# A transformer block in fp32 on one core: the scores of the first key block on 64-row halves of TensorE, interleaved with those of the second

## The chip, the cores and the metric

The kernel runs on one core of a Trainium2 chip. A core has five engines that run side by side and wait for one another by semaphores: TensorE (PE in the profile; its weight loads are listed apart as PEld), VectorE (DVE), ScalarE (ACT), GpSimd (POOL) and SyncE (SP, which here issues the DMAs). The metric is the time of one execution on the device, in microseconds.

## The reference

Sixteen sequences of 256 tokens with 128 features go through a pre-norm block: causal attention with 16 heads (key width 8, value width 64) and then a mixture of 8 experts, in which each expert takes its 64 best tokens of a sequence. What the change touches is the attention:

```python
scores = jnp.einsum('bhqd,bhkd->bhqk', q, k) / scale
causal = jnp.triu(jnp.ones((T, T), dtype=bool), k=1)
scores = jnp.where(causal, jnp.asarray(-jnp.inf, scores.dtype), scores)
attn = jax.nn.softmax(scores, axis=-1)
ctx = jnp.einsum('bhqk,bhkd->bhqd', attn, v)
out = ctx.transpose(0, 2, 1, 3).reshape(B, T, HEADS * D_V)
return out @ Wo
```

## The kernel before, in words

The attention is cut into 64 units: unit `u = 4 b + j` is head group `j` (four heads) of sequence `b`. The work of a unit is spread over several steps of a software pipeline, and every engine has its own program, written out by hand: `batch(b, par)` loops over `j`, and in step `u` the engine works on units `u + 2` to `u - 3`. The order of instructions on an engine is the order in that function; there is no scheduler. Sequences 4 to 9 run in a loop on the device, the others are unrolled.

On TensorE, step `u` of the kernel before does in this order: the scores of the second query block (queries 128 to 255 against all 256 keys) of unit `u + 1`, the query and key products of sequence `b + 2` (only at `j == 3`), the first eight transposes of the probabilities of unit `u - 1` (`turn`), small products of the norms and the gate, the contexts of unit `u - 2`, the output projection of unit `u - 3`, the last four transposes (`turn_last`), the value product of unit `u + 2`, and the scores of the first query block (queries 0 to 127 against keys 0 to 127) of unit `u + 2`. So the first block's scores at the end of one step stand directly ahead of the second block's scores of the same unit at the start of the next.

The scores of four heads come out of one contraction over 128 rows: queries and keys are split into high and low parts, 32 rows a head, and the keys lie in a block diagonal, `k_diag`. The first block is one matmul over all 128 rows with 512 columns, into `s0_ps` (L1276). It adds to the causal mask that VectorE has written there (L892, semaphore `filled0`). The second block is two matmuls over 64 rows each with 512 columns, one on the lower and one on the upper half of the array, for two heads each, into `s1_ps` (L1189), and then four small bf16 matmuls that add the causal mask, also on halves (L1194).

Behind the scores stands this loop: `s0_done` releases VectorE's maximum (L939), this the exponentials of the first block on ScalarE (L529, `exp0`), behind which ScalarE copies transposed probabilities (L538). Those of the second block follow (`s1_done`, maximum L883, L529, `exp1`). TensorE may overwrite `s1_ps` for the next unit only after `exp1`, and `s0_ps` only when VectorE has filled it anew behind `exp0`. The value products, the query and key products and the small products of norms and gate share one tile, `misc_ps0`: each waits until the one before has been copied out (`v_ready`, `qk_lo_done`, `gate_ready`, `x2T_ready`).

Of the kernel before, what the change touches and what calls it, by code (L numbers as in the profile page):

```python
# [13 lines left out]
P = 128  # L14
B, T, D = 16, 256, 128
TB = T // P
H, DK, DV = 16, 8, 64
HG = 4
# [47 lines left out]
def block_kernel(nc, x, w_q, w_k, w_v, w_o, gate_w, w1, w2, out):  # L66
# [3 lines left out]
    with ExitStack() as ctx:  # L70
# [6 lines left out]
        def sem(name):  # L77
            return ctx.enter_context(nc.semaphore(name))
# [149 lines left out]
        v_done = sem("v_done")  # L228
        v_ready = sem("v_ready")
        s0_done = sem("s0_done")  # L230
        s1_done = sem("s1_done")
# [445 lines left out]
        def _(dve):  # L677
# [199 lines left out]
            def batch(b, par):  # L877
                for j in range(G):
# [12 lines left out]
                    if has(u + 2, UNITS) and has(u + 1, UNITS):  # L891
                        nc.vector.tensor_copy(s0_ps[:, :, :], bcast(causal[:, :], 1, HG)).then_inc(filled0, 1)  # L892
                    if j == 0 and has(b + 2, B):
# [12 lines left out]
                    if j == 3 and has(b - 1, B):  # L906
                        norm2_stats(b - 1)
                    if j == 0 and has(b - 2, B):
                        norm2(b - 2)
                    if j == 0 and has(b - 3, B):  # L910
                        if at(u, (44,)):
                            dve.wait_ge(probsT_done[0], 1)
                        copy_gate(b - 3, misc_ps[0])
                        if at(u, (44,)):
                            copy_probs(0, misc_ps[0][0:HALF, T:2 * T])
                    if j == 1 and has(b - 2, B):
# [12 lines left out]
                    if j == 2 and has(b - 2, B):  # L929
                        split_xg(b - 2)  # L930
                    if has(u - 2, UNITS):
                        copy_context(u - 2, r2)
# [97 lines left out]
        def _(pe):  # L1030
# [147 lines left out]
            def batch(b, par):  # L1178
                for j in range(G):
                    u = b * G + j  # L1180
                    r1, r2, rm = (j + 1) % RING, j % RING, (j + 1) % RING
                    if has(u + 1, UNITS):
                        q, kb = (j + 1) % G, par if j < 3 else 1 - par
                        if isinstance(u, int) and u == -1:
                            pe.wait_ge(halves, 10)
                        await_count(pe, exp1, u + 1)
                        tiles = ((slice(0, HALF), 0), (slice(HALF, P), 2))
                        for rows, i in tiles:
                            nc.tensor.matmul(s1_ps[:, i:i + 2, :], qT[kb][rows, q, P:T], k_diag[kb][rows, q, i:i + 2, :],  # L1189
                                             start=True, stop=False, skip_group_check=True)  # L1190
                        for half in range(2):
                            cols = slice(P + half * HALF, P + (half + 1) * HALF)
                            for rows, i in tiles:
                                last = nc.tensor.matmul(s1_ps[:, i:i + 2, cols], half_rows[rows, half, :],  # L1194
                                                        bcast(half_masks[rows, half, :], 1, 2),
                                                        start=False, stop=(half == 1), skip_group_check=True)
                        last.then_inc(s1_done, 1)
                    if j == 3 and has(b + 2, B):
# [8 lines left out]
                        last.then_inc(qk_done, 1)  # L1207
                    if has(u - 1, UNITS):
                        turn(u - 1, rm)
                    if j == 0 and has(b - 3, B):  # L1210
# [55 lines left out]
                    if has(u + 2, UNITS):  # L1266

                        q, kb = (j + 2) % G, par if j < 2 else 1 - par
                        if isinstance(u, int) and u == -2:
                            pe.wait_ge(first_loaded, QK_LOADS)  # L1270
                        elif j == 2 or (isinstance(u, int) and u == -1):
                            pe.wait_ge(qk_loaded, QK_LOADS * (b + 2))
                        await_count(pe, filled0, u + 2)
                        if isinstance(u, int) and u == -2:
                            nc.tensor.matmul(s0_ps[:, :, :], ident_bf[:, :], bcast(causal[:, :], 1, HG), start=True, stop=True)
                        nc.tensor.matmul(s0_ps[:, :, :], qT[kb][:, q, 0:P], k_diag[kb][:, q, :, 0:P], start=False, stop=True,  # L1276
                                         skip_group_check=True).then_inc(s0_done, 1)

# [95 lines left out]
```

## Time and profile before

| | |
|---|---|
| median of 3 runs | 560.72 us (559.99 to 560.88) |
| the profiled execution, its own time | 560.4 us |
| its span from first to last instruction | 558.7 us |
| busy share PE / PEld / DVE / ACT / POOL | 94% / 76% / 74% / 72% / 45% |
| granted clock of TensorE, mean of the span | 0.993 |

The span is the stretch in which the instructions lie; 1.7 us of the execution's own time lie around it. A busy share is a mean over the whole span; attention takes the larger part of it and the experts the rest, and the engines are not loaded alike in the two. Matmuls are pipelined: the start of one is often earlier than the end of the one ahead, so what a matmul costs TensorE is read from start to start, and its own duration tells when its result is there.

### The profile page before, as it was taken

The page shows a single profiled execution, that of the slowest core. Times are in us where ns is not written, and L with a number is a line of the kernel's source. Part 1 is how long each engine was busy: PE and PEld are TensorE (multiplying, and loading weights), DVE is VectorE, ACT ScalarE, POOL GpSimd, SP SyncE. Part 2 cuts the span into 40 slices and gives each one's busy share as a digit, 9 for nine tenths or more (in the row PEclk, how much of TensorE's full clock was granted, in tenths as well). Part 3 has the DMA queues.
Part 4 walks back from the last instruction along what each step waited for, and adds up shares of the span by engine and source line. Part 5 has one row for each costly group of instructions (what it writes and reads, how often), then busy time and mean ns, then how long its engine had stood idle before and what let it go on. Part 6 is the DMA issues. An engine that isn't in the chain of part 4 may idle for free.

```text
span 558.7 us, 13959 instructions
## 1 busy us (share of the span) xinstructions
PE 527.9 (94%) x4777; PEld 427.2 (76%) x4777; DVE 415.7 (74%) x1066; ACT 403.8 (72%) x1383; POOL 253.5 (45%) x249
## 2 busy tenths in 40 slices
PE   1389999999999999999999999999999999999996
PEld 1257777777777877877777777777789998999995
DVE  1477888888888888888898999899873776542354
ACT  4688888888888988989889888889745434334230
POOL 5165555555556556565565565556820101011011
PEclk9979999999999999999999999999999999999999
DMA  4585251732544225042250523410300011000011
GB/s 122 150 211 154 53 151 52 230 118 58 149 117 113 77 73 150 24 126 76 76 149 16 142 76 77 131 22 29 106 21 1 2 39 59 20 21 11 11 29 49
DMA packets 49783, 45.97 MB, mean 82 GB/s; under 512 B 4288, under 2 KB 46528, under 8 KB 49728
## 3 DMA queue, kind: packets, MB, share of 16 engines
q1 hardware_dynamic: 48864, 44.60, 29.2%
q8 instruction: 32, 0.52, 0.4%
q10 hardware_dynamic: 864, 0.66, 0.4%
q14 instruction: 23, 0.19, 0.1%
HBM read 26.35 MB, written 18.89 MB: 81 GB/s over the span
## 4 chain that ended last, share of the span: by engine, by line
PE 90%; ACT 4%; DVE 4%; issue 1%; DMA 1%; POOL 0%; ACTq 0%; DVEq 0%; POOLq 0%
PE ctx_ps L1075 16%; PE misc_ps L1084 12%; PE t_ps L1162 10%; PE t_ps L1048 6%; PE t_ps L1058 5%; PE t_ps L1049 5%; PE s_ps L1189 4%; PE misc_ps L1034 4%; PE s_ps L1146 4%; PE misc_ps L1036 3%; PE misc_ps L1035 3%; PE s_ps L1147 3%; PE s_ps L1148 3%; PE s_ps L1276 3%; PE ctx_ps L1172 2%; ACT prob L529 2%
## 5 line engine op out<-in xcount | busy, mean ns | idle before, releaser
L529 ACT ACTIVATE prob<-s_ps,neg_max 128x128 f32<-128x128 f32 (+1 forms) x512 | 209.9, 437 | 21.2 <-DVE neg_max L939 18.2
L489 POOL TENSOR_TENSOR probn<-prob,inv 128x1024 f32<-128x1024 f32 x64 | 121.2, 1893 | 56.3 <-DVE inv L960 56.3
L529 ACT ACTIVATION_READ_ACCUMULATOR prob<-s_ps,neg_max 128x1 f32 x512 | 114.5, 224 | 0.0
L482 POOL TENSOR_TENSOR probn<-prob,inv 128x512 f32<-128x512 f32 x64 | 66.5, 1040 | 77.7 <-PE t_ps L1058 69.6
L883 DVE TENSOR_REDUCE neg_max<-s_ps 128x4 f32<-128x1024 f32 x64 | 76.4, 1193 | 0.8 <-PE s_ps L1194 0.8
L1084 PE MATMUL misc_ps<-wo_sb,ctxT 128*128 128x128 f32 x512 | 73.9, 287 | 0.7 <-DVE x_all L708 0.7
L506 POOL TENSOR_TENSOR y_parts<-y_sb,y_parts 128x512 fp32r<-128x512 f32 x16 | 20.6, 1287 | 112.6 <-ACT y_parts L587 112.6
L1084 PEld LDWEIGHTS misc_ps<-wo_sb,ctxT 128*128 128x128 f32 x512 | 62.0, 191 | 11.4 <-issue 11.4
L577 ACT ACTIVATE hT<-s_ps 128x512 f32<-128x512 f32 x64 | 38.0, 597 | 44.7 <-PE s_ps L1148 42.2
L1048 PE MATMUL t_ps<-ident,probn 128*128 128x128 f32 x256 | 62.9, 285 | 0.5 <-ACT probT L543 0.5
L1049 PE MATMUL t_ps<-ident,probn 128*128 128x128 f32 x256 | 60.2, 275 | 0.0
L939 DVE TENSOR_REDUCE neg_max<-s_ps 128x4 f32<-128x512 f32 x64 | 44.2, 691 | 18.2 <-PE s_ps L1276 17.5
L753 DVE COPY probT<-t_ps 128x512 f32<-128x512 f32 x64 | 44.1, 690 | 16.8 <-PE t_ps L1058 16.5
L1075 PE MATMUL ctx_ps<-probT,v_odd 128*64 128x256 f32 (+1 forms) x512 | 48.7, 332 | 0.0
L1075 PE MATMUL ctx_ps<-probT,v_even 128*64 128x256 f32 (+1 forms) x512 | 48.7, 332 | 0.0
L747 DVE COPY ctxT<-ctx_ps 128x512 f32<-128x512 f32 x64 | 43.6, 681 | 1.5 <-PE ctx_ps L1075 1.3
L1075 PEld LDWEIGHTS ctx_ps<-probT,v_odd 128*64 128x64 f32 x512 | 31.7, 136 | 14.2 <-issue 4.8
L892 DVE CAST s_ps<-causal 128x512 f32<-128x512 bf16 x63 | 42.4, 673 | 0.0
L1075 PEld LDWEIGHTS ctx_ps<-probT,v_even 128*64 128x64 f32 x512 | 31.7, 136 | 13.8 <-issue 4.4
L543 ACT ACTIVATE probT<-t_ps 128x512 f32<-128x512 f32 x64 | 41.5, 648 | 0.0
L1048 PEld LDWEIGHTS t_ps<-ident,probn 128*128 128x128 f32 x256 | 36.1, 141 | 6.1 <-issue 1.1
L538 ACT ACTIVATE probT<-t_ps 128x512 f32<-128x512 f32 x64 | 39.2, 613 | 0.1
(176 smaller groups left out, 1155.1 us busy)
## 6 DMA issues: line engine op xcount, KB each, us to landing
qT<-q_rows SPq DMA_DIRECT2D x15, 512.0 KB, 4.0
q_rows<-qk_hi SPq DMA_DIRECT2D x32, 128.0 KB, 2.4
q_rows<-qk_lo SPq DMA_DIRECT2D x32, 128.0 KB, 2.4
k_diag_odd<-k_rows SPq DMA_DIRECT2D x32, 128.0 KB, 4.2
k_rows<-qk_hi SPq DMA_DIRECT2D x30, 128.0 KB, 2.4
k_rows<-qk_lo SPq DMA_DIRECT2D x30, 128.0 KB, 2.4
k_diag_even<-k_rows SPq DMA_DIRECT2D x28, 128.0 KB, 4.2
w_raw<-in_L_ffn_w SPq DMA_DIRECT2D x1, 2048.0 KB, 9.5
```

The costliest lines, as they stand in the source:

```text
L482: nc.gpsimd.tensor_tensor(probn[r][:, 0:HG * P].rearrange("p (i k) -> p i k", i=HG), prob[r][:, 0:HG * P].rearrange("p (i k) -> p i k", i=HG),
L489: nc.gpsimd.tensor_tensor(probn[r][:, HG * P:].rearrange("p (i k) -> p i k", i=HG), prob[r][:, HG * P:].rearrange("p (i k) -> p i k", i=HG ...
L529: last = nc.scalar.activation(prob[r][:, first + i * keys:first + (i + 1) * keys], scores[:, i, :], ACT.Exp, bias=neg_max[:, r, block_, i: ...
L747: nc.vector.tensor_copy(ctxT[r][:, :, :], ctx_ps[:, :, :]).then_inc(ctx_ready, 1)
L753: nc.vector.tensor_copy(probT[rm][:, 1024:1536], t_ps[rm][:, :]).then_inc(t_dve, 1)
L883: nc.vector.tensor_reduce(out=neg_max[:, r1, 1, :], in_=s1_ps[:, :, :], axis=AX.X, op=ALU.max, negate=True).then_inc(max1, 1)
L939: nc.vector.tensor_reduce(out=neg_max[:, r2, 0, :], in_=s0_ps[:, :, :], axis=AX.X, op=ALU.max, negate=True).then_inc(max0, 1)
L1048: nc.tensor.transpose(t[:, i, 0:P], q0[:, 2 * f + i, :], ident[:, :])
L1049: last = nc.tensor.transpose(t[:, i, P:T], q1[:, 2 * f + i, 0:P], ident[:, :])
L1075: last = nc.tensor.matmul(ctx_ps[half * DV:(half + 1) * DV, pair, kb * P:T], v_sb[vb][:, kb, h * DV:(h + 1) * DV], rhs, start=(kb == 0), s ...
L1084: last = nc.tensor.matmul(misc_ps[1][:, tb * D:(tb + 1) * D], ctxT[r][:, c, tb * P:(tb + 1) * P], wo_sb[:, 2 * g + c, :], start=(g == 0 an ...
L1162: last = nc.tensor.matmul(y_ps[half * CAP:(half + 1) * CAP, q, :], hT[m % RING][:, half, c, q * CAP:(q + 1) * CAP], w2_of(2 * (m % EP) + h ...
```

## The change

Three edits. First, on TensorE, the scores of the second block move from the start of step `u + 1` to the end of step `u`, which by itself leaves their place behind the first block's as it was; but the first block is now two matmuls on 64-row halves with 256 columns each, and the second block's two matmuls stand between them: first block lower half, second block upper half, second block lower half, first block upper half, then the four mask matmuls. The upper half of the first block waits on a new semaphore, `s0_half`, that the lower half raises when it is complete. The wait for `exp1` stands behind the first of the four. Second, `turn` moves ahead of the query and key products at `j == 3`. Third, on VectorE, the copy of the gate's logits moves to the head of its group at `j == 0`, and the statistics of the second norm move behind the low part of queries and keys at `j == 3`.

```diff
@@ vector, batch
+                    if j == 0 and has(b - 3, B):
+                        if at(u, (44,)):
+                            dve.wait_ge(probsT_done[0], 1)
+                        copy_gate(b - 3, misc_ps[0])
...
-                    if j == 3 and has(b - 1, B):
-                        norm2_stats(b - 1)
...
-                        copy_gate(b - 3, misc_ps[0])
...
+                    if j == 3 and has(b - 1, B):
+                        norm2_stats(b - 1)
@@ tensor, batch
-                    if has(u + 1, UNITS):
-                        q, kb = (j + 1) % G, par if j < 3 else 1 - par
-                        if isinstance(u, int) and u == -1:
-                            pe.wait_ge(halves, 10)
-                        await_count(pe, exp1, u + 1)
-                        tiles = ((slice(0, HALF), 0), (slice(HALF, P), 2))
-                        for rows, i in tiles:
-                            nc.tensor.matmul(s1_ps[:, i:i + 2, :], qT[kb][rows, q, P:T], k_diag[kb][rows, q, i:i + 2, :],
-                                             start=True, stop=False, skip_group_check=True)
...
-                        last.then_inc(s1_done, 1)
+                    if has(u - 1, UNITS):
+                        turn(u - 1, rm)
...
-                    if has(u - 1, UNITS):
-                        turn(u - 1, rm)
...
-                        nc.tensor.matmul(s0_ps[:, :, :], qT[kb][:, q, 0:P], k_diag[kb][:, q, :, 0:P], start=False, stop=True,
-                                         skip_group_check=True).then_inc(s0_done, 1)
+                        if at(u, (-2,)):
+                            nc.tensor.matmul(s0_ps[:, :, :], ident_bf[:, :], bcast(causal[:, :], 1, HG),
+                                             start=True, stop=True).then_inc(s0_half, 1)
+                            pe.wait_ge(s0_half, 1)
+                        tiles = ((slice(0, HALF), 0), (slice(HALF, P), 2))
...
+                        first_block(0).then_inc(s0_half, 1)
+                        await_count(pe, exp1, u + 2)
+                        second_block(1)
+                        second_block(0)
+                        pe.wait_ge(s0_half, u + 4)
+                        first_block(1).then_inc(s0_done, 1)
+                        if at(u, (-2,)):
+                            pe.wait_ge(halves, 10)
+                        for half in range(2):
...
+                        last.then_inc(s1_done, 1)
```

The two new helpers only slice: `first_block(t)` is the matmul of 64 rows into two heads of `s0_ps` (`start=False`, it adds to the mask), `second_block(t)` the one into two heads of `s1_ps`.

On TensorE, at the end of step 2 of a sequence and the start of step 3, the program before reads as follows (names as in the code; a matmul's line is followed by what it writes, what it reads and the semaphores that it waits for):

```order
L1036 MATMUL misc_ps0<-wv_hi,xT_lo0 128x512
L1276 MATMUL s0_ps<-k_diag_even,qT0 128x512 [waits filled0,qk_loaded]
L1189 MATMUL s1_ps<-k_diag_even,qT0 128x512 [waits exp1]
L1189 MATMUL s1_ps<-k_diag_even,qT0 128x512
L1194 MATMUL s1_ps<-half_masks,half_rows 128x2x64 x4
L1034 MATMUL misc_ps0<-xT_hi1,wqk_hi 128x256 [waits v_ready,xT_ready]
```

The same place in the changed program:

```order
L1037 MATMUL misc_ps0<-wv_hi,xT_lo0 128x512
L1268 MATMUL s0_ps<-k_diag_even,qT0 128x256 [waits filled0,qk_loaded]
L1274 MATMUL s1_ps<-k_diag_even,qT0 128x512 [waits exp1]
L1274 MATMUL s1_ps<-k_diag_even,qT0 128x512
L1268 MATMUL s0_ps<-k_diag_even,qT0 128x256 [waits s0_half]
L1288 MATMUL s1_ps<-half_masks,half_rows 128x2x64 x4
L1049 MATMUL t_ps0<-ident,probn0 128x128 [waits t_act,normed]
```

The one matmul with 512 columns has become two with 256, the second of them behind `exp1` and `s0_half`, and the transposes follow the masks where the query and key products stood.

On VectorE, the steps 3 and 0 before, from the fill of the mask (L892) on:

```order
L892 CAST s0_ps<-causal 128x512
L680 MEMSET holds_wait 128x1
L682 BN_STATS bn6<-x_all 128x6 x2
L685 MEMSET holds_wait 128x1 [waits bn1_done]
L687 BN_AGGR mv1<-bn6 128x2 x2
L692 TENSOR_SCALAR xn2<-x_all,mv2,rstd2 128x128 [waits xg_lo_done,x2T_done,rstd2_done]
L692 TENSOR_SCALAR xn2<-x_all,mv2,rstd2 128x128
L727 COPY gate_logit<-misc_ps0 128x16 [waits gate_done]
```

and of step 0 now:

```order
L893 CAST s0_ps<-causal 128x512
L728 COPY gate_logit<-misc_ps0 128x16 [waits gate_done]
L681 MEMSET holds_wait 128x1
L683 BN_STATS bn6<-x_all 128x6 x2
L686 MEMSET holds_wait 128x1 [waits bn1_done]
L688 BN_AGGR mv1<-bn6 128x2 x2
```

The copy of the logits, which frees `misc_ps0` for the next value product, has moved ahead of the statistics and of the norm.

## Rows read from the trace of the kernel before

**Rows 1.** Busy time by engine of 50 to 360 us, with clock and DMA:
```profile
core 0: us, PE busy (x) PEld busy (x) DVE busy (x) ACT busy (x) POOL busy (x), PEclk, DMA share, GB/s
50.00:360.00 310.00, 310.00 (x2610) 240.35 (x2610) 267.84 (x679) 272.40 (x1044) 178.39 (x158) 1.00 0.37 101
```
**Rows 2.** Who waited for whom, whole span: us in total, times, longest us:
```profile
PEld s_ps L1189 <- issue: 22.1, 59, 0.7
ACT prob L529 <- DVE neg_max L939: 18.2, 45, 1.0
DVE neg_max L939 <- PE s_ps L1276: 17.5, 58, 2.7
```
**Rows 3.** Timeline, end of step 2: start us, us, engine, line, operation:
```profile
254.13 0.27 ACT L529 ACTIVATION_READ_ACCUMULATOR prob<-s_ps,neg_max 128x1 f32 x1
...
254.54 0.39 PE L1036 MATMUL misc_ps<-wv_hi,xT_lo 128*128 128x512 f32 x1
...
254.77 0.40 PE L1276 MATMUL s_ps<-k_diag_even,qT 128*128 128x512 f32 x1
254.97 0.60 ACT L631 ACTIVATE v_even<-misc_ps 128x512 f32<-128x512 f32 x1
255.09 0.19 PEld L1189 LDWEIGHTS s_ps<-k_diag_even,qT 64*128 64x128 f32 x2 [0.37 <-issue]
...
255.20 0.69 DVE L939 TENSOR_REDUCE neg_max<-s_ps 128x4 f32<-128x512 f32 x1 [0.24 <-PE s_ps L1276]
255.43 0.12 PEld L1194 LDWEIGHTS s_ps<-half_masks,half_rows 64*128 64x128 bf16 x4 [0.15 <-issue]
...
255.65 0.39 PE L1034 MATMUL misc_ps<-xT_hi,wqk_hi 128*128 128x256 f32 x1
...
255.88 0.28 PE L1035 MATMUL misc_ps<-xT_lo,wqk_hi 128*128 128x256 f32 x1
...
256.00 0.28 PE L1036 MATMUL misc_ps<-xT_hi,wqk_lo 128*128 128x256 f32 x1
```
**Rows 4.** Timeline, VectorE's copies of `misc_ps0` ahead of value products, steps 1 and 0:
```profile
247.32 0.42 DVE L734 COPY xn2T<-misc_ps 128x256 f32<-128x256 f32 x1
...
248.27 0.19 PEld L1034 LDWEIGHTS misc_ps<-wv_hi,xT_hi 128*128 128x128 f32 x1
...
265.57 0.17 DVE L727 COPY gate_logit<-misc_ps 128x16 f32<-128x16 f32 x1
...
266.05 0.19 PEld L1034 LDWEIGHTS misc_ps<-wv_hi,xT_hi 128*128 128x128 f32 x1
```
**Rows 5.** Timeline, the first units, from the first score on:
```profile
22.98 0.65 PE L1275 MATMUL s_ps<-causal,ident_bf 128*128 128x512 bf16 x1
...
23.07 0.99 PE L1276 MATMUL s_ps<-k_diag_even,qT 128*128 128x512 f32 x1
...
24.95 0.57 PE L1034 MATMUL misc_ps<-xT_hi,wqk_hi 128*128 128x256 f32 x1
...
27.86 0.47 PE L1034 MATMUL misc_ps<-wv_hi,xT_hi 128*128 128x512 f32 x1 [1.74 <-DVE qk_lo L924]
...
32.15 0.76 PE L1276 MATMUL s_ps<-k_diag_even,qT 128*128 128x512 f32 x1 [1.68 <-DVE s_ps L892]
...
32.88 0.24 ACT L529 ACTIVATION_READ_ACCUMULATOR prob<-s_ps,neg_max 128x1 f32 x1
...
33.17 0.29 PEld L1189 LDWEIGHTS s_ps<-k_diag_even,qT 64*128 64x128 f32 x2 [0.76 <-ACT prob L529]
...
33.68 0.37 ACT L529 ACTIVATE prob<-s_ps,neg_max 128x128 f32<-128x128 f32 x1
...
33.76 0.18 PEld L1194 LDWEIGHTS s_ps<-half_masks,half_rows 64*128 64x128 bf16 x4 [0.30 <-issue]
...
35.94 0.72 PEld L1058 LDWEIGHTS t_ps<-ident,probn 128*128 128x128 f32 x4 [0.23 <-ACT probT L538]
```
**Rows 6.** Timeline, a late unit, while VectorE also searches the experts' tokens:
```profile
366.67 0.21 ACT L529 ACTIVATION_READ_ACCUMULATOR prob<-s_ps,neg_max 128x1 f32 x1
...
367.26 0.19 PEld L1189 LDWEIGHTS s_ps<-k_diag_even,qT 64*128 64x128 f32 x2 [0.36 <-ACT prob L529]
```

More of the change, by code:

```diff
@@ L229, in block_kernel @@
         v_ready = sem("v_ready")
+        s0_half = sem("s0_half")
         s0_done = sem("s0_done")
@@ L892, in batch @@
                         nc.vector.tensor_copy(s0_ps[:, :, :], bcast(causal[:, :], 1, HG)).then_inc(filled0, 1)
+                    if j == 0 and has(b - 3, B):
+                        if at(u, (44,)):
+                            dve.wait_ge(probsT_done[0], 1)
+                        copy_gate(b - 3, misc_ps[0])
+                        if at(u, (44,)):
+                            copy_probs(0, misc_ps[0][0:HALF, T:2 * T])
                     if j == 0 and has(b + 2, B):
@@ L905, in batch @@
                         norm(xn1, lambda tb: x_all[:, (b + 2) * TB + tb, :], mv1, rstd1, xn1_ready)
-                    if j == 3 and has(b - 1, B):
-                        norm2_stats(b - 1)
                     if j == 0 and has(b - 2, B):
                         norm2(b - 2)
-                    if j == 0 and has(b - 3, B):
-                        if at(u, (44,)):
-                            dve.wait_ge(probsT_done[0], 1)
-                        copy_gate(b - 3, misc_ps[0])
-                        if at(u, (44,)):
-                            copy_probs(0, misc_ps[0][0:HALF, T:2 * T])
                     if j == 1 and has(b - 2, B):
@@ L1181, in batch @@
                     r1, r2, rm = (j + 1) % RING, j % RING, (j + 1) % RING
-                    if has(u + 1, UNITS):
-                        q, kb = (j + 1) % G, par if j < 3 else 1 - par
-                        if isinstance(u, int) and u == -1:
-                            pe.wait_ge(halves, 10)
-                        await_count(pe, exp1, u + 1)
-                        tiles = ((slice(0, HALF), 0), (slice(HALF, P), 2))
-                        for rows, i in tiles:
-                            nc.tensor.matmul(s1_ps[:, i:i + 2, :], qT[kb][rows, q, P:T], k_diag[kb][rows, q, i:i + 2, :],
-                                             start=True, stop=False, skip_group_check=True)
[L1191 to L1196, printed above, removed]
-                        last.then_inc(s1_done, 1)
+                    if has(u - 1, UNITS):
+                        turn(u - 1, rm)
                     if j == 3 and has(b + 2, B):
@@ L1273, in batch @@
                         await_count(pe, filled0, u + 2)
-                        if isinstance(u, int) and u == -2:
-                            nc.tensor.matmul(s0_ps[:, :, :], ident_bf[:, :], bcast(causal[:, :], 1, HG), start=True, stop=True)
-                        nc.tensor.matmul(s0_ps[:, :, :], qT[kb][:, q, 0:P], k_diag[kb][:, q, :, 0:P], start=False, stop=True,
-                                         skip_group_check=True).then_inc(s0_done, 1)
+                        if at(u, (-2,)):
+                            nc.tensor.matmul(s0_ps[:, :, :], ident_bf[:, :], bcast(causal[:, :], 1, HG),
+                                             start=True, stop=True).then_inc(s0_half, 1)
+                            pe.wait_ge(s0_half, 1)
@@ new lines, in batch, with first_block, second_block @@
+                        tiles = ((slice(0, HALF), 0), (slice(HALF, P), 2))
+                        def first_block(t):
+                            rows, i = tiles[t]
+                            return nc.tensor.matmul(s0_ps[:, i:i + 2, :], qT[kb][rows, q, 0:P], k_diag[kb][rows, q, i:i + 2, 0:P],
+                                                    start=False, stop=True, skip_group_check=True)
+                        def second_block(t):
+                            rows, i = tiles[t]
+                            nc.tensor.matmul(s1_ps[:, i:i + 2, :], qT[kb][rows, q, P:T], k_diag[kb][rows, q, i:i + 2, :],
+                                             start=True, stop=False, skip_group_check=True)
@@ new lines, in batch @@
+                        first_block(0).then_inc(s0_half, 1)
[7 more added lines that the diff above has]
+                        for half in range(2):
+                            cols = slice(P + half * HALF, P + (half + 1) * HALF)
+                            for rows, i in tiles:
+                                last = nc.tensor.matmul(s1_ps[:, i:i + 2, cols], half_rows[rows, half, :],
+                                                        bcast(half_masks[rows, half, :], 1, 2),
+                                                        start=False, stop=(half == 1), skip_group_check=True)
```

## The prediction

> **What bounds the kernel now.** I read the busy time by stretches first. From 50 to 360 us TensorE is busy 310.00 of 310.00 us at a granted clock of 1.00, ScalarE 272.40 and VectorE 267.84 [rows 1]. So in attention the time is what TensorE issues from start to start, and the other two follow it with 12% and 14% to spare. The list of waits comes second: the weight load of the second block's scores stands idle 59 times, 22.1 us together, with no releaser ("issue"), which is TensorE's own cost of going over to 64 rows. VectorE's maximum waits for the first block's scores 58 times and ScalarE's exponentials for that maximum 45 times [rows 2]. So the first block's scores start the chain of the other engines in nearly every unit: whatever delays them delays both engines. The timeline shows the order inside one unit [rows 3].
>
> **The stretch that is replaced.** From the start of the last value matmul to the first matmul behind the masks TensorE takes 255.65 - 254.54 = 1.11 us, in four pieces: 0.23 for the value matmul, 0.32 for the first block's scores and the going over to 64 rows, 0.34 for the second block's pair (its weight load stands in the open), 0.22 for the masks and going back [rows 3].
>
> **The same stretch after the change.**
> 1. The value matmul (512 columns, 128 rows) is now itself followed by a 64-row matmul, as the first block's was: 0.32. The first half of the first block starts then, 0.09 later than L1276 did.
> 2. The upper half of the first block waits until the lower half is complete. Complete is not when its columns are in: a matmul of 256 columns whose weight load stands in the open lasts 0.39 (L1034), and the maximum L939 starts 0.03 behind the end of L1276, so the end is when a semaphore is raised [rows 3]. TensorE itself wakes 0.05 behind what it waits for: ScalarE's last read ends at 33.12, the load of L1189 starts at 33.17 [rows 5]. So the second half starts 0.39 + 0.05 = 0.44 behind the first. The second block's pair runs in these 0.44; like its 0.34 before, it fits.
> 3. The upper half's load is behind the wait, so it stands in the open: 0.39 - 0.28 = 0.11, and its 256 columns take 0.12 (L1035 to L1036). The masks do not overlap it: before, their load began only when the second block's columns were in, 0.34 = 0.11 + 0.23. So 0.11 + 0.12 = 0.23 [rows 3].
> 4. Masks and going back, unchanged: 0.22.
>
> The sum is 0.32 + 0.44 + 0.23 + 0.22 = 1.21, against 1.11: **0.10 more for each unit**. Put otherwise, 0.23 for the columns of L1276 and 0.34 for the pair go, and 0.44 and 0.23 come. The trace of before has no matmul that waits for one of TensorE's own, so piece 2 has bounds: from below, the upper half is free when the second block's upper matmul has its columns in, 0.34, which makes the stretch 1.11 (no change); with the weights loaded meanwhile, 1.00. From above, the wait is longer by the 0.08 between the end of the value copy L631 (255.57) and L1034 that waits for it (255.65), instead of 0.05: 1.24 [rows 3]. I take 1.21, since both parts of 0.44 are rows of the same kind. For the 59 units that stand in a row on a busy TensorE [rows 2]: 59 x 0.10 = **+5.9 us**, bounds -6.5 and +7.7.
>
> **What is late next.** `s0_done` comes with the upper half: first half's start + 0.44 + 0.39, that is 254.86 + 0.83 = 255.69 instead of 255.17, **0.52 later** in every unit. The maximum and the exponentials that waited anyway [rows 2] go with it. Three places where TensorE waits for them:
> - `exp1`: done at 254.40, needed at 255.09, a slack of 0.69 [rows 3]. Now it is needed 0.23 earlier and comes 0.52 later, while a unit is 0.10 longer: 0.04 left. It still holds, barely. This was a step 2, where ScalarE has an extra conversion; it is the tightest of the four.
> - the value product in step 1 waits for VectorE's copy: 247.74 against 248.27, 0.53; 0.53 + 0.10 - 0.52 leaves 0.11 [rows 4].
> - in step 0 it waits for the gate's copy, 265.74 against 266.05: 0.31, which would be used up. Here the third edit answers: the copy moves ahead of statistics and norm and comes some 1 us earlier. It costs nothing by itself; without it step 0 would lose about 0.1.
>
> The other moves I count at nothing. The query and key products start behind eight transposes, and ScalarE's conversion of them stands behind the 0.52 later exponentials, which cover most of that. VectorE's low part follows at once now, since the statistics were moved behind it; who waits for these, GpSimd's scale, has a step in hand. The products no longer stand directly behind `v_ready`, which was 0.08 ahead of L1034: a gain of hundredths in 16 steps. No DMA is moved past another.
>
> **The start** is a chain, not a busy TensorE. In the first unit the mask matmul must now complete before the first half (22.98 + 0.65 + 0.05), then come two halves of 0.57 (the length of L1034 there, which has 256 columns and its load in the open too) with 0.05 between: `s0_done` at 24.87 instead of 24.06, +0.81 [rows 5]. The next value product waits for what follows on ScalarE and VectorE (1.74 before L1034), so it moves along; the second unit adds the 0.52: +1.33. In the third, `exp1` is what TensorE waits for: last read ends at 33.12, now 34.45, load at 34.50. The first block's upper half now stands behind this wait; before, the whole first block did not. It starts 0.59 later (L1189's load to L1194's), ends 0.57 after that, at 35.66, where the first block was complete at 32.91. The exponentials that began at 33.68, at once behind the maximum, go by the same 2.75, and the transposes at 35.94 waited for what stands behind them [rows 5]. So the start costs **+2.8 us** up to the fifth unit, between 1.3 (if the third unit's second delay is absorbed) and 3.5.
>
> **The end of attention.** In the units 59 to 63 VectorE also searches tokens, and the slack of `exp1` is less: 366.88 against 367.26 [rows 6], 0.38, so by the same sum 0.38 + 0.10 - 0.75 = -0.27. Two or three such units: **+0.6 us** (0 to 1.2). The experts behind are untouched.
>
> **The sum:** 560.4 (own time of the profiled execution) + 2.8 + 5.9 + 0.6 = 569.7. The median of the runs is 0.3 above that execution, so I say **569.8 us**.
>
> **One rule weighed.** The row is that the load of L1189 started 0.05 behind the last read it waited for, so a weight load stands behind its wait [rows 5]. The Trainium skill, "TensorE: Matmul & The Clock Gate", Part 3, The mechanism, says that TensorE pulls a weight load ahead of running matmuls where the row groups differ. By it the upper half's load would lie inside the 0.44, the stretch would be 1.10, and the time 563.2 or so. No row here shows a load pulled past an unmet wait, so the sum goes without it.
>
> **Rivals.**
> - *The wait costs little* (0.13): the lower half completes earlier on 64 rows than L1034 does on 128, or the load is done ahead. The stretch is 1.10 to 1.11, only start and end cost: 560.4 + 2.5 + 0.6 = 563.5. For it: no 64-row matmul of 256 columns is in the trace. Against it: L1276's end and L939 fit to 0.03.
> - *The interleaving pays* (0.12): the upper half is loaded and free when the second block's columns are in, 0.34 behind the first half. The stretch is 0.32 + 0.34 + 0.12 + 0.22 = 1.00, 59 x -0.11 = -6.5; with the start at +2.5 and the end +0.6: 557.0. It decides the sign when the second half follows the first by less than about 0.28 with its load in the open, since the start must be earned back too.
> - *Two engines become the bound* (0.10): the slack of 0.04 in step 2 and 0.11 in step 1 is gone if `s0_done` is 0.2 later than worked out. Then half of the units wait some 0.2 more: 30 x 0.2 = 6, 575.7.
>
> **How the numbers follow.** My forecast has 0.62 (566.5 to 573); 0.03 is left for cases that I don't see. The range of 561.5 to 574.5 holds it and the first rival, and leaves out the second and most of the third. About 0.2% (1.1 us) is what this measurement can tell from no change. Faster than that is the second rival less its dear half, 0.11; within it the seam of the first two, 0.05; slower the rest, 0.84.
>
> **What would show it.** In the changed trace, in the middle: the second L1268 starts 0.44 behind the first; L1036's successor L1037 to the first transpose is 1.21; the maximum L940 moves from 0.66 to about 1.2 behind the start of that value matmul; the idle of ScalarE ahead of L529 grows or stays; the load of the second block never or hardly waits for `exp1` in the middle, and does in the third unit. The prediction is wrong if the second L1268 starts within 0.34 of the first, or if value products in step 1 or second-block loads in step 2 are released by VectorE and ScalarE in every round.

## The result, and the profile after

The changed kernel takes **569.73 us** (median of 4 runs, 569.34 to 571.33) beside 560.8 of the kernel before on the same chip: a ratio of **1.0168 [1.0148, 1.0188]**. 569.8 was forecast. The profiled execution spans 567.5 us, before 558.7. The next sections show that several of the terms behind the sum were off, in opposite directions, so that the closeness is partly luck.

The list of waits of the changed kernel (us in total, times, longest), with the lines that answer to [rows 2]:

```profile
ACT prob L530 <- DVE neg_max L940: 49.7, 62, 1.9
...
DVE neg_max L940 <- PE s_ps L1268: 46.5, 61, 3.5
...
PEld s_ps L1268 <- issue: 23.1, 62, 0.7
...
PEld s_ps L1274 <- ACT prob L530: 1.1, 2, 0.7
```

VectorE's maximum and ScalarE's exponentials wait nearly three times as long as before, 46.5 and 49.7 against 17.5 and 18.2, in nearly every unit. TensorE's own cost of going over to 64 rows, the "issue" line, is as large as before, 23.1 against 22.1. It now stands ahead of the first block's first half. The second block waits for `exp1` twice.

Busy time over the stretch of [rows 1]:

```profile
50.00:360.00 310.00, 309.70 (x2630) 242.44 (x2628) 260.10 (x663) 266.95 (x1031) 174.36 (x155) 1.00 0.36 99
```

TensorE still reads as busy, 309.70 of 310.00 us at a granted clock of 1.00. The loss shows in the count: 2630 matmuls, of which some 52 are the one that each unit has more. That leaves 2578 where 2610 fitted before. A semaphore wait that lies beside another running matmul does not show as idle time here.

The end of a step 2 (start us, us), the place of [rows 3]:

```profile
260.53 0.40 PE L1037 MATMUL misc_ps<-wv_hi,xT_lo 128*128 128x512 f32 x1
260.56 0.26 ACT L530 ACTIVATION_READ_ACCUMULATOR prob<-s_ps,neg_max 128x1 f32 x1
...
260.85 0.18 PEld L1268 LDWEIGHTS s_ps<-k_diag_even,qT 64*128 64x128 f32 x1 [0.36 <-issue]
260.86 0.38 PE L1268 MATMUL s_ps<-k_diag_even,qT 64*128 64x256 f32 x1
260.88 0.27 PEld L1274 LDWEIGHTS s_ps<-k_diag_even,qT 64*128 64x128 f32 x2
...
261.30 0.18 PEld L1268 LDWEIGHTS s_ps<-k_diag_even,qT 64*128 64x128 f32 x1
...
261.31 0.32 PEld L1288 LDWEIGHTS s_ps<-half_masks,half_rows 64*128 64x128 bf16 x4
...
261.72 0.69 DVE L940 TENSOR_REDUCE neg_max<-s_ps 128x4 f32<-128x512 f32 x1 [0.75 <-PE s_ps L1268]
...
261.74 0.14 PEld L1049 LDWEIGHTS t_ps<-ident,probn 128*128 128x128 f32 x1
```

From the last value matmul to the first transpose it is 261.74 - 260.53 = 1.21, before 1.11. The pieces: 0.32 to the first half's load, 0.45 to the second's, and 0.44 for that half, the masks and the going back. The second half's load begins only here, though the pair's load, the last one ahead of it in TensorE's order, ended at 261.15. VectorE's maximum starts 1.19 behind the value matmul, before 0.66.

In step 1, the place of the first pair in [rows 4], the value product's load now stands right behind VectorE's copy:

```profile
253.64 0.42 DVE L735 COPY xn2T<-misc_ps 128x256 f32<-128x256 f32 x1
...
254.17 0.19 PEld L1035 LDWEIGHTS misc_ps<-wv_hi,xT_hi 128*128 128x128 f32 x1
```

That is 0.11 behind the copy's end, before 0.53. It is 0.11 to 0.12 in 8 of 14 rounds.

The start, the place of [rows 5]:

```profile
22.27 0.65 PE L1260 MATMUL s_ps<-causal,ident_bf 128*128 128x512 bf16 x1
...
22.98 0.58 PE L1268 MATMUL s_ps<-k_diag_even,qT 64*128 64x256 f32 x1
...
23.62 0.58 PE L1268 MATMUL s_ps<-k_diag_even,qT 64*128 64x256 f32 x1
...
34.60 0.24 ACT L530 ACTIVATION_READ_ACCUMULATOR prob<-s_ps,neg_max 128x1 f32 x1
...
34.89 0.29 PEld L1274 LDWEIGHTS s_ps<-k_diag_even,qT 64*128 64x128 f32 x2 [0.73 <-ACT prob L530]
35.06 0.33 PEld L1268 LDWEIGHTS s_ps<-k_diag_even,qT 64*128 64x128 f32 x1
...
36.66 0.37 ACT L530 ACTIVATE prob<-s_ps,neg_max 128x128 f32<-128x128 f32 x1 [1.33 <-DVE neg_max L940]
...
38.70 0.71 PEld L1059 LDWEIGHTS t_ps<-ident,probn 128*128 128x128 f32 x4 [1.07 <-ACT probT L539]
```

In the third unit the pair waits for the last read of `exp1` (34.60 + 0.24, load at 34.89), the upper half stands behind it, and the first exponential starts at 36.66. Before, the same one started at 33.68, 2.98 earlier; the transposes are 2.76 later.

To place the time, I cut the span at the start of the last value matmul of the 6th, the 59th and the 64th unit, in the changed kernel these rows:

```profile
53.14 0.40 PE L1037 MATMUL misc_ps<-wv_hi,xT_lo 128*128 128x512 f32 x1
...
368.15 0.40 PE L1037 MATMUL misc_ps<-wv_hi,xT_lo 128*128 128x512 f32 x1
...
398.99 0.40 PE L1037 MATMUL misc_ps<-wv_hi,xT_lo 128*128 128x512 f32 x1
```

The same four stretches of all traces, us; the experiments are explained in the next section:

| kernel | start | middle, 53 units | last five units | behind | span |
|---|---|---|---|---|---|
| before | 49.84 | 311.18 | 29.98 | 167.69 | 558.7 |
| changed | 53.14 | 315.01 | 30.84 | 168.54 | 567.5 |
| e1_whole (moves alone) | 49.73 | 309.87 | 28.96 | 168.32 | 556.9 |
| e2_halves_only | 53.74 | 321.32 | 31.93 | 168.37 | 575.4 |
| e4_start | 52.11 | 315.08 | 30.83 | 168.25 | 566.3 |
| e5_masks_ahead | 53.88 | 311.09 | 31.02 | 168.25 | 564.2 |
| e6_vector_back | 52.88 | 319.71 | 31.93 | 168.14 | 572.7 |
| e7_products_back | 53.45 | 317.44 | 30.84 | 168.28 | 570.0 |
| e8_start_whole | 49.02 | 315.04 | 30.84 | 168.32 | 563.2 |
| e9_longer_wait | 55.32 | 327.46 | 31.86 | 168.61 | 583.3 |

Against before the change costs 3.3 at the start, 3.8 in the middle, 0.9 in the last five units and 0.85 behind. The stretch behind is 0.45 to 0.9 longer than in that one trace of before in every other kernel, whatever its edit; I did not follow it.

### The profile page after: what moved, and what is told of

The parts are those of the page before. It is cut to its first block, busy times and chain, and to the rows that moved or that the text cites. A ratio compares the mean times of both kernels' runs of the same rounds, so it can differ in the third digit from the quotient of the medians.

```text
span 567.5 us, 14105 instructions
## 1 busy us (share of the span) xinstructions
PE 536.3 (94%) x4841; PEld 436.5 (77%) x4841; DVE 412.5 (73%) x1066; ACT 401.6 (71%) x1383; POOL 252.8 (45%) x249
## 4 chain that ended last, share of the span: by engine, by line
PE 84%; DVE 6%; ACT 5%; issue 2%; DMA 2%; POOL 1%; ACTq 0%; DVEq 0%; POOLq 0%
PE ctx_ps L1076 15%; PE misc_ps L1085 11%; PE t_ps L1163 9%; PE t_ps L1049 6%; PE t_ps L1059 5%; PE t_ps L1050 4%; PE s_ps L1268 4%; PE misc_ps L1035 3%; PE s_ps L1147 3%; PE misc_ps L1037 3%; PE misc_ps L1036 3%; ACT prob L530 3%; PE s_ps L1274 3%; PE s_ps L1288 2%; PE s_ps L1148 2%; PE s_ps L1149 2%
## 5 line engine op out<-in xcount | busy, mean ns | idle before, releaser
L530 ACT ACTIVATE prob<-s_ps,neg_max 128x128 f32<-128x128 f32 (+1 forms) x512 | 209.9, 438 | 51.9 <-DVE neg_max L940 49.7
L940 DVE TENSOR_REDUCE neg_max<-s_ps 128x4 f32<-128x512 f32 x64 | 44.2, 691 | 46.7 <-PE s_ps L1268 46.5
L1049 PE MATMUL t_ps<-ident,probn 128*128 128x128 f32 x256 | 64.6, 291 | 1.3 <-ACT probT L544 0.6
L1050 PE MATMUL t_ps<-ident,probn 128*128 128x128 f32 x256 | 60.9, 277 | 0.0
L544 ACT ACTIVATE probT<-t_ps 128x512 f32<-128x512 f32 x64 | 41.5, 648 | 0.0
L1059 PE MATMUL t_ps<-ident,probn 128*128 128x128 f32 x256 | 39.0, 275 | 0.7 <-ACT probT L539 0.7
```

The lines of the kernel that those rows point to most:

```text
L530: last = nc.scalar.activation(prob[r][:, first + i * keys:first + (i + 1) * keys], scores[:, i, :], ACT.Exp, bias=neg_max[:, r, block_, i: ...
L940: nc.vector.tensor_reduce(out=neg_max[:, r2, 0, :], in_=s0_ps[:, :, :], axis=AX.X, op=ALU.max, negate=True).then_inc(max0, 1)
L1049: nc.tensor.transpose(t[:, i, 0:P], q0[:, 2 * f + i, :], ident[:, :])
L1050: last = nc.tensor.transpose(t[:, i, P:T], q1[:, 2 * f + i, 0:P], ident[:, :])
L1059: last = nc.tensor.transpose(t[:, i, :], q1[:, i, P:T], ident[:, :])
```

## The experiments

Diffs are against the changed kernel. Ratios are to the kernel before on the same chip, with 95% intervals; a ratio's distance from the changed kernel's 1.0168 says what the edit is worth.

**e1_whole.** The moves alone: the first block is one matmul on 128 rows again, ahead of the wait for `exp1`; the copies, statistics and products stay moved.

```diff
-                        first_block(0).then_inc(s0_half, 1)
+                        nc.tensor.matmul(s0_ps[:, :, :], qT[kb][:, q, 0:P], k_diag[kb][:, q, :, 0:P], start=False, stop=True,
+                                         skip_group_check=True).then_inc(s0_done, 1)
                         await_count(pe, exp1, u + 2)
-                        second_block(1)
                         second_block(0)
-                        pe.wait_ge(s0_half, u + 4)
-                        first_block(1).then_inc(s0_done, 1)
+                        second_block(1)
```

> The moves alone: the first block is one matmul over 128 rows again, ahead of the second block's pair; the transposes stay ahead of the query and key products and VectorE's two moves stay. If the halves and their wait are the whole cost, the stretch from the last value matmul to the first matmul behind the masks is 1.11 us again and the time 559.5 to 561.0, at or a little under the kernel before, since the changed trace has step 3 only 0.04 longer where the others are 0.08 to 0.10 longer. Rival, the moves carry part of the cost: 563 or more.

Measured: 558.18 us, **0.9951 [0.9935, 0.9968]**, below the expected range. From the last value matmul to the first transpose it is 1.11 to 1.12 again, so the halves and their wait are what made the stretch longer. The moves are a gain of some 2.4 us by themselves, and this kernel beats both. The table shows where: 1.3 in the middle and 1.0 in the last five units. The second is mostly one wait: a value product of before stood 0.8 for VectorE's copy of the gate's logits. The line is in the waits of before,

```profile
PE misc_ps L1034 <- DVE gate_logit L727: 0.8, 1, 0.8
```

and is gone with the copy moved. Of the first, 0.9 is in step 3: its median period (from one last value matmul to the next) falls from 6.273 to 6.204, 0.04 to 0.18 in each of 13 rounds. The other 0.4 is in step 0, where three rounds of before are 0.13 to 0.15 longer than in e1. One of them:

```profile
218.79 0.17 DVE L727 COPY gate_logit<-misc_ps 128x16 f32 x1
...
219.07 0.19 PEld L1034 LDWEIGHTS misc_ps<-wv_hi,xT_hi 128*128 128x128 f32 x1
```

The load stands 0.11 behind the copy's end there, so TensorE already waited for it before the change; in e1 the copy comes earlier and these rounds take 5.84.

**e2_halves_only.** The halves alone: VectorE's order and the products' place are as before (the edits of e6 and e7 together).

> The halves alone: interleaved halves with their wait, but the query and key products ahead of the transposes and VectorE's order as before. If the moves give a little back, 570 to 573 us (the gate's copy comes too late in step 0 by about 0.1, 14 times, and step 3 is 0.05 longer). If the moves cost something: 568 or less.

Measured: 577.23 us, **1.0293 [1.0265, 1.0321]**, above the whole expected range. Without the moves the halves cost 16.6 us, with them 11.5 (569.73 - 558.18). So under the halves the moves are worth 7.5, three times as much as alone.

**e6_vector_back, e7_products_back.** The two parts of it. In the first only VectorE's order is undone:

```diff
-                    if j == 0 and has(b - 3, B):
...
-                        copy_gate(b - 3, misc_ps[0])
...
+                    if j == 3 and has(b - 1, B):
+                        norm2_stats(b - 1)
                     if j == 0 and has(b - 2, B):
                         norm2(b - 2)
+                    if j == 0 and has(b - 3, B):
...
+                        copy_gate(b - 3, misc_ps[0])
...
-                    if j == 3 and has(b - 1, B):
-                        norm2_stats(b - 1)
...
```

> The changed kernel with VectorE's two moves undone (gate's copy behind the norm, statistics ahead of the low part of queries and keys); the transposes stay ahead of the query and key products. With all moves undone the time was 577.2, 7.5 more than the changed kernel; the step 0 was 0.27 longer and the step 3 0.22. If the gate's copy is what step 0 lost and the order of transposes and products what step 3 lost, step 0 loses its 0.27 here and step 3 little: 573 to 575 us. Rival, all of it comes from the products ahead of the transposes: 570 us.

Measured: 574.74 us, **1.026 [1.0243, 1.0277]**. In the trace of e6, in step 0:

```profile
274.59 0.17 DVE L728 COPY gate_logit<-misc_ps 128x16 f32<-128x16 f32 x1
...
274.87 0.19 PEld L1035 LDWEIGHTS misc_ps<-wv_hi,xT_hi 128*128 128x128 f32 x1 [0.21 <-issue]
```

The value product's load follows the copy's end by 0.11 and stood idle 0.21 ahead of it. In the changed kernel the same two rows are 1.06 apart, end to start:

```profile
270.95 0.16 DVE L728 COPY gate_logit<-misc_ps 128x16 f32<-128x16 f32 x1
...
272.17 0.19 PEld L1035 LDWEIGHTS misc_ps<-wv_hi,xT_hi 128*128 128x128 f32 x1
```

Step 0 takes 6.17 on the mean in e6 and 5.92 in the changed kernel, 0.01 to 0.59 more from round to round: over its 14 rounds 3.6 of the 4.7 that e6 is longer in the middle. Step 3 has 0.9 of the rest, 0.6 of it in a single round. The last five units add 1.1, the start and the stretch behind take 0.7 back; the medians are 5.0 apart.

In e7 only the query and key products go back ahead of the transposes:

```diff
-                    if has(u - 1, UNITS):
-                        turn(u - 1, rm)
                     if j == 3 and has(b + 2, B):
...
                         last.then_inc(qk_done, 1)
+                    if has(u - 1, UNITS):
+                        turn(u - 1, rm)
```

> The changed kernel with only the query and key products put back ahead of the transposes; VectorE's moves stay. They wait for the copy of the value product, which is late now that ScalarE's exponentials are: step 3 is 0.2 longer, 15 times, and the rest as in the changed kernel: 572 to 574 us. Rival, the 7.5 us are VectorE's alone: 570 us.

Measured: 571.81 us, **1.0205 [1.0188, 1.0222]**, 2.1 more than the changed kernel and a little under the expected range. In step 3 of e7:

```profile
262.43 0.40 PE L1037 MATMUL misc_ps<-wv_hi,xT_lo 128*128 128x512 f32 x1
...
263.03 0.67 ACT L632 ACTIVATE v_even<-misc_ps 128x512 f32<-128x512 f32 x1
...
263.81 0.19 PEld L1035 LDWEIGHTS misc_ps<-xT_hi,wqk_hi 128*128 128x128 f32 x1 [0.28 <-issue]
```

The products write to the tile that ScalarE's value copy L632 reads, `misc_ps0`. The copy starts 0.60 behind its value matmul (262.43); before, it was 0.43 [rows 3]. ScalarE comes to it behind exponentials that are later than before: their last read starts 0.03 behind that matmul (262.46), before it was 0.41 ahead of it (254.13). The products start 0.11 behind its end, and the stretch is 1.38 instead of 1.21.

**e5_masks_ahead.** The upper half's two masks run ahead of the wait for the lower half, the lower ones behind the upper half of the first block.

```diff
                         second_block(0)
+                        mask(0, 1)
+                        mask(1, 1)
                         pe.wait_ge(s0_half, u + 4)
                         first_block(1).then_inc(s0_done, 1)
...
-                        for half in range(2):
...
-                        last.then_inc(s1_done, 1)
+                        mask(0, 0)
+                        mask(1, 0).then_inc(s1_done, 1)
```

> The changed kernel, but the two mask matmuls of the upper half stand ahead of the wait for s0_half, and those of the lower half behind the first block's upper half, so that the array has work while it waits. If the idle wait is the cost: the second L1268 still starts 0.44 behind the first, but the next 128-row matmul comes 0.30 behind it instead of 0.44, the stretch is 1.07 and the time 561 to 563 us. Rival, the cost is in the half-width matmuls or in going between fp32 and bf16 weights on a half: the stretch stays at 1.20 or grows, 569 to 573 us.

Measured: 566.18 us, **1.0098 [1.007, 1.0126]**, 3 us above the expected range. TensorE's loads in a unit:

```profile
152.25 0.19 PEld L1037 LDWEIGHTS misc_ps<-wv_hi,xT_lo 128*128 128x128 f32 x1
152.80 0.18 PEld L1268 LDWEIGHTS s_ps<-k_diag_odd,qT 64*128 64x128 f32 x1 [0.36 <-issue]
152.80 0.29 PEld L1274 LDWEIGHTS s_ps<-k_diag_odd,qT 64*128 64x128 f32 x2
153.14 0.11 PEld L1281 LDWEIGHTS s_ps<-half_masks,half_rows 64*128 64x128 bf16 x2
153.24 0.18 PEld L1268 LDWEIGHTS s_ps<-k_diag_odd,qT 64*128 64x128 f32 x1
...
153.55 0.14 PEld L1049 LDWEIGHTS t_ps<-ident,probn 128*128 128x128 f32 x1
```

The second half is 0.44 behind the first, as without the edit, and the transposes follow it by 0.31 instead of 0.44. The masks now lie in the wait. That is 0.12 to 0.13 less in a unit, but the median periods show it in two of the four steps only: step 0 falls by 0.12 (5.919 to 5.800) and step 2 by 0.12 (5.787 to 5.666); step 1 goes from 5.805 to 5.809 and step 3 from 6.288 to 6.277. In step 1 the value product waits for VectorE's copy of `misc_ps0`, the rows of [rows 4] in e5:

```profile
157.20 0.41 DVE L735 COPY xn2T<-misc_ps 128x256 f32<-128x256 f32 x1
...
157.73 0.19 PEld L1035 LDWEIGHTS misc_ps<-wv_hi,xT_hi 128*128 128x128 f32 x1
```

157.61 to 157.73 is 0.12, the same as in e6 behind the gate's copy, where the load certainly waited. The other place is the end of step 2, with which the period of step 3 begins. There the pair waits for `exp1`, whose last read ends at 164.38:

```profile
164.12 0.26 ACT L530 ACTIVATION_READ_ACCUMULATOR prob<-s_ps,neg_max 128x1 f32 x1
...
164.27 0.18 PEld L1268 LDWEIGHTS s_ps<-k_diag_even,qT 64*128 64x128 f32 x1 [0.36 <-issue]
164.42 0.19 PEld L1274 LDWEIGHTS s_ps<-k_diag_even,qT 64*128 64x128 f32 x2
```

The pair stands 0.15 behind the first half instead of 0.03. So a shorter stretch on TensorE is worth little more than half here (3.9 us in the middle, where 53 x 0.125 would be 6.6): the other two engines hold the unit in the other steps.

**e9_longer_wait.** The signal to the upper half is given by the second block's lower half, so that it comes later.

```diff
-                        first_block(0).then_inc(s0_half, 1)
+                        first_block(0)
...
-                        second_block(0)
+                        second_block(0).then_inc(s0_half, 1)
```

> The changed kernel, but the semaphore that the upper half waits for is raised by the second block's lower half, which completes some 0.2 later, so that the same wait is longer and nothing else differs. If TensorE stands idle in this wait, the second L1268 starts 0.66 behind the first, the stretch is 1.42, 59 times 0.22 is 13 us more, and the exponentials that follow are so late that step 2 waits for exp1 as well: 582 to 590 us. Rival, the wait is covered by the second block's pair and the cost is in the half-width matmuls: 569 to 572 us.

Measured: 584.97 us, **1.0446 [1.0424, 1.0468]**. Its loads:

```profile
253.07 0.18 PEld L1268 LDWEIGHTS s_ps<-k_diag_odd,qT 64*128 64x128 f32 x1 [0.37 <-issue]
253.07 0.29 PEld L1274 LDWEIGHTS s_ps<-k_diag_odd,qT 64*128 64x128 f32 x2
253.75 0.18 PEld L1268 LDWEIGHTS s_ps<-k_diag_odd,qT 64*128 64x128 f32 x1 [0.38 <-PE s_ps L1274]
254.19 0.14 PEld L1049 LDWEIGHTS t_ps<-ident,probn 128*128 128x128 f32 x1
```

0.68 instead of 0.44 between the halves, and each of the 53 units of the middle is 0.235 longer (327.46 - 315.01): the wait is on the path with its whole length, in every step. What follows the upper half stays 0.44.

**e4_start, e8_start_whole.** Two edits in the first five units only. In e4 the upper half stands ahead of the wait for `exp1`; in e8 the first block is whole there, and the wait for the mask matmul of the first unit goes with the halves (e1 keeps it).

```diff
+                        early = at(u, (-2, -1, 0, 1, 2))
+                        if early:
+                            pe.wait_ge(s0_half, u + 4)
+                            first_block(1).then_inc(s0_done, 1)
                         await_count(pe, exp1, u + 2)
...
-                        pe.wait_ge(s0_half, u + 4)
-                        first_block(1).then_inc(s0_done, 1)
+                        if not early:
+                            pe.wait_ge(s0_half, u + 4)
+                            first_block(1).then_inc(s0_done, 1)
```

> The changed kernel, but in the first five units the first block's upper half stands ahead of the wait for exp1 (fixed place in the program, the loop is untouched). If the third unit's second delay is that the upper half stands behind exp1, the start is 1.2 to 1.6 us shorter: 568.1 to 568.5 us, and the middle is as in the changed kernel. Rival, the start's 3.3 us come from the mask matmul's completion and from the halves alone: no change, 569.7.

> The changed kernel, but in the first five units the first block is one matmul over 128 rows, ahead of the wait for exp1. If the start's 3.4 us all come from the halves, the waits for them and their place behind exp1, they are gone: 566.2 to 566.8 us, and the rest of the trace is as in the changed kernel. Putting the upper half ahead of exp1 alone gave 1.0 us of it. Rival, part of the start comes from the moved instructions: 567.5 or more.

Measured: e4 567.94 us, **1.0135 [1.0101, 1.0169]**; e8 565.54 us, **1.0098 [1.0076, 1.012]**. Both are a little under what was expected. By the table the halves and the mask's wait cost 4.1 at the start (53.14 - 49.02); e4, where the upper half is no longer behind `exp1`, gives back 1.0 of it. The middle is the changed kernel's in both (315.08, 315.04), so the start is a loss of its own.

Halves of the first block in two separate tiles, without a wait between them, were not tried, so what the halves cost without their wait is not shown.

## Why the prediction was right, and where not

The forecast was right to 0.1 us, and its parts were not all right. The last step has a slip: 569.7 and the 0.3 by which the median lies above the profiled execution are 570.0, not 569.8. The halves' own cost is the changed kernel less e1, the moves' that of e1 less before:

| term | forecast | measured, from the table |
|---|---|---|
| halves, middle | 53 x 0.10 = 5.3 | 315.01 - 309.87 = 5.1 |
| halves, start | 2.8 | 53.14 - 49.73 = 3.4 (by e8: 4.1) |
| halves, last five units | 5 x 0.10 + 0.6 = 1.1 | 30.84 - 28.96 = 1.9 |
| moves | 0 | -1.3 in the middle, -1.0 in the last five units |

**The stretch** came out as worked out: 1.21, second half 0.44 behind the first, 0.097 in a unit. e9 shows that this wait is on the path: 0.24 more between the halves makes each unit 0.235 longer. Both of the gentle rivals fall with it: the wait isn't short, and the upper half's load is not done ahead. The Trainium skill's rule on that, "TensorE: Matmul & The Clock Gate", Part 3, The mechanism, says that a weight load is pulled ahead where row groups differ. The trace agrees where nothing is waited for: the loads of L1268 and L1274, on different halves, are 0.03 apart. No load in it is pulled past an unmet wait: the upper half's begins at 261.30, though the load ahead of it ended at 261.15.

**What is late next.** `s0_done` is 0.53 later, 0.52 was forecast. The slacks were counted from the end of the producer, and the step failed there by one latency: the rows of e6 and e7 have 0.11 from the end of a copy to the load that waited for it. With it the gate's copy in step 0 has 0.31 - 0.11 + 0.10 - 0.52 = -0.22, not -0.1, and in the round that [rows 4] shows e6 is 0.23 longer than the changed kernel. That round is also one of the roomiest: in three of the middle's rounds before, the load stood 0.11 to 0.12 behind the copy, as at 219.07, which gives -0.41, and there e6 is 0.35 to 0.59 longer. The value product in step 1 has 0.53 - 0.11 + 0.10 - 0.52 = 0.00 left, not 0.11. `exp1` in step 2 has 0.69 - 0.05 + 0.10 - 0.75 = -0.01, so none, not 0.04. The changed kernel does run with no slack at both places: the value product's load in step 1 is 0.11 behind its copy (254.17), and the pair's in step 2 is 0.06 behind the last read of `exp1` (260.82 to 260.88). That is near the prediction's own sign of being wrong, which asked for it in every round. The rival of two engines that become the bound costs it only hundredths in the middle (step 1 takes 5.79 to 5.82) but begins at once behind it: e5 loses nearly half its gain to just these two.

**The moves counted at nothing** are the step that was wrong. "Costs nothing by itself" was true of their price. Their gain was looked for only as an answer to the halves. Alone they give 1.0 in the last five units, most of it at one wait of before that stood in the list, 0.8 for `gate_logit`; 0.4 in three step 0 for the same copy; and 0.9 over 13 step 3, the "hundredths" of the prediction. Not all of these are the wait for `v_ready`: where the products' load stood 0.11 behind the value copy, step 3 mostly took 6.27 to 6.28, elsewhere 6.25, and with the products moved 6.20. The 0.05 that is left comes with the new order, and I did not follow it. Beside the halves they hide more: 5.0 by VectorE's order (e6), 2.1 by the products' place (e7). I had put down as cover there that the products' conversion on ScalarE stands behind late exponentials. What was late was ScalarE's value copy, which the products would have waited for.

**The start** came out at 3.4 where 2.8 was forecast, and that closeness is luck in part. In the first unit the maximum starts 0.13 later than before and not 0.81, since the mask matmul itself ran 0.71 earlier in this execution. In the third the exponentials go by 2.98, and 2.75 was forecast. But 1.14 of the 2.98 is not the halves': e1, which has none, starts the same exponential at 34.82. It is not the moves' either: in the second unit the maximum is at 29.06 before and at 30.17 in e1, but with the halves it is at 30.79 beside the moves and at 30.90 without them (e2). What differs is TensorE's clock. The same product before and in e1:

```profile
25.48 0.28 PE L1036 MATMUL misc_ps<-xT_hi,wqk_lo 128*128 128x256 f32 x1
...
25.52 0.41 PE L1037 MATMUL misc_ps<-xT_hi,wqk_lo 128*128 128x256 f32 x1
```

0.28 is its length in the middle too, at a granted clock of 1.00 (2.4 GHz) [rows 3]. In the trace of before TensorE was then busy 3.78 of the 7.20 us from 25.0 to 32.2, and the granted clock fell to 0.50 (1.2 GHz) until 39.0, in the columns of [rows 1]:

```profile
32.20:39.00 6.80, 6.54 (x25) 4.43 (x25) 4.97 (x14) 6.41 (x25) 4.78 (x5) 0.50 0.73 197
```

A transpose lasts 0.42 in that stretch and 0.27 behind it. By these lengths TensorE is at the lower level in the changed kernel until 44, and in e1 only until 38:

```profile
43.54 0.42 PE L1050 MATMUL t_ps<-ident,probn 128*128 128x128 f32 x1
...
39.83 0.27 PE L1050 MATMUL t_ps<-ident,probn 128*128 128x128 f32 x1
```

The traces' first entries of a granted clock, both 1.00, stand at 44.06 and 38.11; ahead of them the profile has none and prints 1.00. From 32.2 to 39.0 TensorE is busy 4.38 us in the changed kernel and 5.89 in e1. The stretch from the fourth to the fifth unit's value matmul takes 6.38 in the changed kernel and 4.77 in e1: 1.6 of the 3.4 arise there, which the prediction did not have, while up to the third unit the halves cost less than forecast (36.66 - 34.82 = 1.84). That the clock makes all of the 1.6 is not shown.

**The last five units** cost the halves 1.9 and not 1.1. The pair waits for `exp1` in one of them, as in [rows 6]:

```profile
380.15 0.18 PEld L1268 LDWEIGHTS s_ps<-k_diag_odd,qT 64*128 64x128 f32 x1 [0.36 <-issue]
...
380.69 0.19 PEld L1274 LDWEIGHTS s_ps<-k_diag_odd,qT 64*128 64x128 f32 x2 [0.36 <-ACT prob L530]
```

The pair is 0.54 behind the first half, where 0 to 0.03 is the rule and a wait of 0.27 in two or three units was worked out; the transposes come 0.34 later by it. The prediction had no term for the rest. Against e1, the output projection of the same step stands 0.43 longer for VectorE's `x_all`, a value product in step 1 comes 0.32 later, with its load 0.12 behind VectorE's copy, and transposes come 0.28 later behind VectorE's `probT`. So VectorE does become a bound here.

So halves that cost more than forecast (10.4 over the three stretches against 9.2) met moves that gained 2.3 where nothing was forecast. With 0.85 behind, which no step had, the sum came out. The stretch and its wait were understood; that the total fits to 0.1 us is luck.

## What to carry to other kernels

Two matmuls that must follow each other by a semaphore are not interleaved for free: TensorE pays from the start of the first to its completion, 0.44 us here, and the second's weight load stands in the open behind that. Count a slack from the end of the producer plus the time that its waiter needs to start; the 0.11 left out here was the difference between slack and none. Take it from the tightest round of a loop, not from one round that is at hand. Where a change has several parts, run each alone: the part that was there to help was the only one that made the kernel faster (0.9951). Where two traces differ in a stretch that is not yet busy, compare the lengths of the same matmul first: the clock may differ, and not the program.

## What the runs showed of the hardware

- A matmul of 64 rows and 256 columns that waits for one of TensorE's own starts 0.44 us behind it, as worked out from matmuls on 128 rows. At the start, where the same matmul lasts 0.58 instead of 0.38, it is 0.64 (22.98 to 23.62).
- A load that waits for a VectorE or ScalarE copy starts 0.11 to 0.12 behind the copy's end (e5, e6, e7); behind ScalarE's last read of a sum it is 0.04 to 0.05 (164.38 to 164.42 in e5, 34.84 to 34.89 in the changed kernel).
- TensorE reads as busy 310.00 of 310.00 us without and 309.70 with a 0.44 wait in every unit. The count of matmuls and the period of the loop show it.
- The granted clock can fall again during the start: before, it was 0.50 from 32.2 to 39.0, a transpose lasted 0.42 instead of 0.27, and the third unit lay in it.
